# Moving an SBUF layout from multiples of 32 bytes to multiples of 64: four graph layers on one core

## The reference

```python
# layer 0, twice: relational convolution, 8 relations over 4 bases
m = sum(comp[etype, b] * norm * (h @ basis[b])[src] for b in bases)
out = segment_sum(m, dst) + bias + h @ loop_w
# layer 1: the same form, 32 relations over 8 bases
# layer 2: mean of the neighbours through W2, own row through W1
# layer 3, 4 blocks of:
y = (x - mu) * rsqrt(var + eps) * (1 + cond @ sw + sb) + cond @ bw + bb
q, k, v = y @ wq + bq, y @ wk + bk, y @ wv + bv     # 4 heads of 128
x = x + softmax_over_edges(q[src] . k[dst]) v[dst] @ wo + bo
y = norm(x) as above with its own weights
x = x + relu(y @ m_w1 + m_b1) @ m_w2 + m_b2
```

## Time and profile before

| | |
|---|---|
| median of three runs | 3153.47 us (3148.95, 3153.47, 3154.17) |
| profiled execution, first to last instruction (span) | 3143.3 us |
| PE busy | 94% of the span |
| VectorE, ScalarE, GpSimd busy | 66%, 41%, 38% |
| mean granted clock | 0.988 |

### The profile page before, as it was taken

The page is one execution under the profiler, slowest core; times in us unless marked ns, Lnnn a source line. Parts: engine busy times, 40 slices in busy tenths (PEclk is TensorE's granted clock), DMA queues, the critical chain, the costliest instruction groups (busy, mean ns, idle before and its releaser), DMA issues.

```text
span 3143.3 us, 42911 instructions
## 1 busy us (share of the span) xinstructions
PE 2966.4 (94%) x14658; PEld 2176.8 (69%) x14658; DVE 2076.1 (66%) x5081; ACT 1275.2 (41%) x2245; POOL 1178.9 (38%) x938
## 2 busy tenths in 40 slices
PE   5898998999979899999999999999999999999999
PEld 2333774445843357875458998889987999879987
DVE  7999224886358763444376677567766776767677
ACT  4666431002340033342254554355543555435554
POOL 4666336664456643432022123511135102431022
PEclk8999999999989999999999999999999999999999
DMA  2555524664246542333012001310113001130012
GB/s 80 166 168 161 166 96 136 171 173 143 81 131 179 169 124 89 95 99 121 12 45 88 15 31 50 101 43 8 37 57 118 14 8 65 44 104 15 8 64 80
DMA packets 129593, 279.31 MB, mean 89 GB/s; under 512 B 22742, under 2 KB 45590, under 8 KB 128354
## 3 DMA queue, kind: packets, MB, share of 16 engines
q0 software_dynamic: 40320, 132.15, 14.8%
q1 hardware_dynamic: 87618, 141.76, 14.2%
q10 hardware_dynamic: 1440, 2.62, 0.2%
HBM read 227.85 MB, written 27.48 MB: 81 GB/s over the span
## 4 chain that ended last, share of the span: by engine, by line
PE 74%; DVE 13%; another core or an unknown queue 6%; ACT 3%; issue 2%; DMA 2%; POOL 1%; DVEq 0%; SPq 0%; POOLq 0%; ACTq 0%
PE bank L155 16%; PE bank L157 16%; PE bank L156 16%; PE bank L889 9%; PE bank L2545 5%; PE bank L2209 3%; PE bank L1849 2%; PE bank L860 2%; DVE G L996 2%; DVE onehot_dst L963 1%; DVE y_tile L2161 1%; DVE y_tile L2163 1%; DVE x_stats L2144 1%; DMA yT_lo<-yT_new_lo 1%
## 5 line engine op out<-in xcount | busy, mean ns | idle before, releaser
L889 PE MATMUL bank<-gathered,selector 128*128 x1328 | 641.5, 606 | 57.7 <-SPq L848 30.9
L996 DVE TENSOR_TENSOR G<-G,bank 128x512 f32 x664 | 450.4, 678 | 23.5 <-PE bank L889 23.3
L889 PEld LDWEIGHTS bank<-gathered,selector 128*128 128x128 f32 x1328 | 231.8, 192 | 303.8 <-issue 167.2
L2633 ACT CAST probT<-bank 128x512 fp32r<-128x512 f32 (+2 forms) x480 | 212.2, 515 | 263.0 <-PE bank L2545 262.1
L1510 POOL TENSOR_TENSOR weight_parts<-weight_ring,weight_parts 128x512 fp32r<-128x512 f32 x130 | 188.0, 1446 | 296.7 <-ACT weight_parts L1443 296.6
L2715 DVE CUSTOM_DVE_ANT_0 prob<-bank,count_by_src 128x512 f32<-128x512 f32 (+1 forms) x480 | 258.4, 589 | 58.8 <-PE bank L157 58.8
L1469 DVE TENSOR_TENSOR lhs_parts<-G,lhs_parts 128x640 fp32r<-128x640 f32 x122 | 102.3, 840 | 288.4 <-ACT lhs_parts L1441 288.2
L2641 DVE TENSOR_TENSOR probT<-bank,probT 128x512 fp32r<-128x512 f32 (+2 forms) x480 | 254.0, 585 | 52.1 <-ACT probT L2633 51.3
L870 ACT COPY G<-bank 128x512 f32<-128x512 f32 x160 | 82.3, 654 | 492.2 <-remote 405.2
L155 PE MATMUL bank<-weight_parts,lhs_parts 128*128 128x512 f32 x680 | 268.7, 395 | 11.3 <-POOL weight_parts L1510 5.5
L157 PE MATMUL bank<-weight_parts,lhs_parts 128*128 128x512 f32 x680 | 266.5, 392 | 0.0
(11 more groups left out here) (295 smaller groups left out, 6807.5 us busy)
## 6 DMA issues: line engine op xcount, KB each, us to landing
weight_ring<-in_L_gnn_basis SPq DMA_DIRECT2D x64, 256.0 KB, 2.7
weight_ring<-in_L_gnn_bases SPq DMA_DIRECT2D x64, 256.0 KB, 2.7
x_L<-x_rows SPq DMA_DIRECT2D x50, 256.0 KB, 4.4
x_rows<-x_L SPq DMA_DIRECT2D x50, 256.0 KB, 5.8
yT_hi<-yT_new_hi SPq DMA_DIRECT2D x4, 2560.0 KB, 11.4
yT_lo<-yT_new_lo SPq DMA_DIRECT2D x4, 2560.0 KB
count_rows<-count SPq DMA_DIRECT2D x10, 642.0 KB, 5.7
count_by_dst<-count_rows SPq DMA_DIRECT2D x10, 642.0 KB, 4.6
```

The lines of the kernel that those rows point to most:

```text
L889: ins = pe.matmul(bank[s % banks][:], sel[:, s % SELECTORS, :], tile_rows_of[s % BATCH], start=True, stop=True)
L996: ins = dve.tensor_tensor(g, g, bank[s % banks][:], ALU.add)
L2633: ins = act.copy(hi, of)
```

## The change

The allocator rounds the start of every tensor of 256 bytes or more, and of every tensor made by `new_split`, up to a multiple of 64. `C.after_small` is rounded too. In layer 3 the ten tensors of small columns become slices of one tensor, `columns`, of 136 words per partition; `C.rows_place` becomes a multiple of 64, with probT first and prob behind it. `tile_of_step` and `steps_of_tile` (and the scratch `tile_int`) hold 2-byte instead of 4-byte entries; `window_of_step` stays at 4 bytes. No instruction is added, removed or reordered in the source.

```diff
 class Arena:
...
         self.n += 1
+        if size >= 256:
+            self.align()
         t = self.nc.alloc_sbuf_tensor_at(f"{name}_{self.n}", shape, dtype, offset=self.at)
...
+    def align(self):
+        self.at = -(-self.at // 64) * 64
+        return self.at
+
     def new_split(self, name, shape):
 
+        self.align()
         at = self.at
...
-    C.after_small = M.at
+    C.after_small = M.align()
...
-    C.tile_of_step = {PATH1: M.new("tile_of_step", [1, PATH1.steps // BATCH, 2, BATCH], I32)}
-    C.steps_of_tile = {PATH1: M.new("steps_of_tile", [1, T], I32)}
+    C.tile_of_step = {PATH1: M.new("tile_of_step", [1, PATH1.steps // BATCH, 2, BATCH], U16)}
+    C.steps_of_tile = {PATH1: M.new("steps_of_tile", [1, T], U16)}
...
-    C.tile_of_step[PATH0] = M.new("tile_of_step", [1, PATH0.steps // BATCH, 2, BATCH], I32)
-    C.steps_of_tile[PATH0] = M.new("steps_of_tile", [1, T], I32)
+    C.tile_of_step[PATH0] = M.new("tile_of_step", [1, PATH0.steps // BATCH, 2, BATCH], U16)
+    C.steps_of_tile[PATH0] = M.new("steps_of_tile", [1, T], U16)
...
-    tile_i = M.new("tile_int", [1, PATH1.steps], I32)
+    tile_i = M.new("tile_int", [1, PATH1.steps], U16)
...
-    C.rows_place = (M.end - 4 * (2 * N + 4 + 2 * NT * 4 * P)) // 32 * 32
+    C.rows_place = (M.end - 64 - 4 * (2 * N + 2 * NT * 4 * P)) // 64 * 64
...
-    stats = M.new("x_stats", [P, NT, 6])
-    means = M.new("x_mean_var", [P, NT, 2])
...
-    rsum = M.new("row_sum", [P, 2, NT])
+    columns = M.new("columns", [P, 10 * NT + 6 + KC + 6 + 2 * NT])
+    stats = columns[:, 0:6 * NT].rearrange("p (j a) -> p j a", a=6)
+    means = columns[:, 6 * NT:8 * NT].rearrange("p (j a) -> p j a", a=2)
...
+    hb, rmax, nmax = (columns[:, 10 * NT + 2 * a:10 * NT + 2 * a + 2] for a in range(3))
...
+    rsum = columns[:, 10 * NT + 12 + KC:].rearrange("p (h t) -> p h t", h=2)
...
-    prob = M.new("prob", [P, 2, N])
     PT = M.new("probT", [P, 2, 2, NT, QUERIES], F32R)
+    prob = M.new("prob", [P, 2, N])
```

More of the change, by code:

```diff
@@ L6 @@
 F32R = mybir.dt.float32r
-F32, I32, BF16, F16 = mybir.dt.float32, mybir.dt.int32, mybir.dt.bfloat16, mybir.dt.float16
+F32, I32, U16, BF16, F16 = mybir.dt.float32, mybir.dt.int32, mybir.dt.uint16, mybir.dt.bfloat16, mybir.dt.float16
 ALU = mybir.AluOpType
@@ L1966, in layer_3 @@
     modw = M.new("modulation_parts", [STACKED, 2, D], F32R)
-    stats = M.new("x_stats", [P, NT, 6])
-    means = M.new("x_mean_var", [P, NT, 2])
-    rstds = M.new("x_rstd", [P, NT, 1])
-    shifts = M.new("x_shift", [P, NT, 1])
-    hb = M.new("head_bias_cols", [P, 2])
-    mb = M.new("mlp_bias_cols", [P, KC])
-    rmax = M.new("row_max", [P, 2])
-    nmax = M.new("negated_max", [P, 2])
-    smax = M.new("span_max", [P, 2, 3])
-    rsum = M.new("row_sum", [P, 2, NT])
+    columns = M.new("columns", [P, 10 * NT + 6 + KC + 6 + 2 * NT])
+    stats = columns[:, 0:6 * NT].rearrange("p (j a) -> p j a", a=6)
+    means = columns[:, 6 * NT:8 * NT].rearrange("p (j a) -> p j a", a=2)
+    rstds = columns[:, 8 * NT:9 * NT].rearrange("p (j a) -> p j a", a=1)
+    shifts = columns[:, 9 * NT:10 * NT].rearrange("p (j a) -> p j a", a=1)
+    hb, rmax, nmax = (columns[:, 10 * NT + 2 * a:10 * NT + 2 * a + 2] for a in range(3))
+    mb = columns[:, 10 * NT + 6:10 * NT + 6 + KC]
+    smax = columns[:, 10 * NT + 6 + KC:10 * NT + 12 + KC].rearrange("p (s n) -> p s n", s=2)
+    rsum = columns[:, 10 * NT + 12 + KC:].rearrange("p (h t) -> p h t", h=2)
     V_hi = M.new("value_parts_hi", [P, 2, NP], F32R)
@@ L1987, in layer_3 @@
     M.at = heads_only = C.rows_place
+    PT = M.new("probT", [P, 2, 2, NT, QUERIES], F32R)
     prob = M.new("prob", [P, 2, N])
-    PT = M.new("probT", [P, 2, 2, NT, QUERIES], F32R)
     end_of_heads = M.at
```

## The result

The kernel after takes 3178.68 us (median of 6 runs, 3170.34 to 3185.15), the kernel before 3153.82 us beside it (6 runs, 3148.95 to 3161.01): ratio 1.0078, 95% interval 1.0063 to 1.0092. The forecast was 3145.5 us, faster than before, with a range of 3138.5 to 3154.5. The profiled execution of after took 3175.8 us and its span is 3174.4, 31.1 us more than before's. That is more than the 24.9 us between the medians. With the 1.4 us that lie around after's span, before's profiled execution took about 3144.7 us (an estimate), 9 us under the median of its kernel.

A forecast was written before the change was run, and what follows sets the result against it. PE was taken as the bound, busy 94% of the span, mostly split products in layer 3. PE's terms summed to -8.5 us; 90%, -8 us, from 3153.5 gave 3145.5 us, range 3138.5 to 3154.5.

The forecast's parts named there:

- Term 13: Two-byte tables, read as registers on PE and POOL in the gathers: same number of loads, taken at 0.
- register loads get dearer: Rival, PE's queue in the three gathers: dearer 2-byte loads make the kernel slower, 3170 us at 15% coming through; chance 0.06.
- Terms 1, 2 and 3: Layer 3's 512-wide projections from yT, value projections and hidden layer: aligning the one odd operand gains 3.5, 2.9 and 2.5 us.
- Terms 4 and 5: Layer 3's output products and 512-wide scores, both operands odd: alignment saves 3.1 ns per matmul, 3.0 us each.
- Term 6: Modulation by condT, 160 matmuls with both operands odd: gain between 0 and 1.1 us, taken as -0.5 us.
- Term 7: 256-wide matmuls: aligned pairs are slower, +5.6 us at the value products and +0.8 us at projections from yT.
- Term 8: The 226-wide matmuls, some 1300: between -3.5 and +3.8 us, taken as +0.5 us.
- Term 9: fp32 products (gathers, transposes, layer 2): G, gathered and selector stay at multiples of 64, bounds 0 either side.
- Term 10: ScalarE's 512-wide casts, 590 to 570 ns when aligned: beside PE, so taken as 0, with -1 us as other end.
- Terms 11 and 12: Copies (PE's 3.1 us wait for yT_lo) and the shared tensor of small columns: both taken at 0.
- the prediction's own signs of being wrong: Wrong if the gain lies outside layer 3, or layer 3 shortens by under 4 or over 12 us.
- address is not the cause: Rival: 227 against 233 ns hangs on relative place or SBUF row and survives the shift; 3153.5 us, no change; chance 0.18.

The follow-up runs named there:

- align_only: The kernel after with its tables put back to 4 bytes and one more register operation before PE's and POOL's waits against loaded values: ratio 1.0014 to before.
- held: The kernel before, 4-byte tables, with one more register operation in front of each PE and POOL wait against a loaded value: ratio 1.0019 to before.

## Why the prediction was wrong

- **Term 13, the tables, is the step that failed in size and sign of the whole.** It took 0, "since a load of four values stays one instruction". It does stay one, but lasts 985 ns instead of 329. The tables alone cost 1.4% on one chip, and PE's alone about 1% on another. The rival "register loads get dearer" had the place (PE's queue in the gathers), its sign came true (the gathers grow and PE's idle time is put down to issue), and at 15% coming through it had 3170 us. That this is only 9 us off is partly luck. It supposed loads twice as long, which would be 332 x 329 ns = 109 us more, and worked with 167 us, an idle time and not a load time; the loads became three times as long, 218 us more, and 14% of that came through. Its chance of 0.06 rested on the count of instructions and on VectorE's table staying at 4 bytes. The rows of 4-byte loads were in the trace and bound them at 329 ns; one load per value at the worst would have been 4 x 329 ns, 1.3 us, which is above what came.
- **Terms 1, 2 and 3** (8.9 us together for one odd operand) failed in cause. The distances went from 233.2 to 233.0, 233.3 to 232.4 and 233.2 to 232.6 ns, under 1 us in sum. The 6 ns were real, but belong to two operands whose rests by 256 differ; a shift that leaves them different keeps them. The rows at 227 ns had both tensors at the same rest by 256, not merely both at 64: 192 for yT_new and head_weights, and in the transforms weight_parts and lhs_parts both at 128 in layer 0 and both at 64 in layer 1.
- **Terms 4 and 5** (3.1 ns for both odd): 229.9 to 229.7 and 230.8 to 230.9. These pairs agree by 256 before and after and still are not at 227; in the trace most of their distances lie between 224 and 236. What lengthens them is open, and so is whether the rule is all that counts inside the kernel.
- **Term 6** (modulation, -0.5 us) is too small to be read. The 48 distances under 300 ns that the trace has before give 236.5 ns, the 44 after 233.2; but four over 260 ns make that difference, and without them it is 233.5 and 233.2.
- **Term 7** (+6.4 us) had the wrong sign: 117.4 to 116.6 ns at the value products, -1.6 us, and 117.3 to 115.3 at the projections. The shift of probT against V_hi and V_lo changed their rests (224 against 192 and 224, then 128 against 64 and 0); that this is the cause was not shown. **Term 8** (+0.5): 111.5 to 111.7 ns, right. Term 9: 429 ns as before, right.
- **Term 10**: the cast stays at 590 ns; the 20 ns against the cast into yT_new are not the address. It was taken at nothing for the end, so no harm was done. **Terms 11 and 12** at 0: PE's wait for yT_lo is 3.2 instead of 3.1 us, and align_only, which has the shared columns, is no slower than held.
- **The sum** of what layer 3 gained is 3.5 us, and was taken as 8; under 4 us was one of the prediction's own signs of being wrong. The rival "address is not the cause" named the tensors' place relative to each other, which is what was found at 512 columns; it was weighed at 0.18 against rows that could not tell the two apart, since every aligned pair in them was also an agreeing one. The Trainium skill's "Advanced Engine Details and Errata", section SBUF Cachelines, has lines of 16 bytes, from which the prediction worked out that 32 against 64 does nothing. The runs agree in that both operands 32 bytes on cost nothing, and that a moving operand 4 bytes on is the slowest (236.9 ns); the 6 ns between rests by 256 are not in that rule.

## What to carry to other kernels

Before an index table is narrowed, ask who reads it: as a register load, four 4-byte values cost PE 334 ns and four 2-byte values 984. Where an engine's queue is near full, a part of the time of its register loads comes through to the end (14% of 218 us here), and single register operations in front of its waits cost too (0.2% in held). In this kernel one load of eight 4-byte values with the operations packed behind it gave that back. For split products of 512 columns compare the rests by 256 of the two operands' addresses, not each address alone (4 to 5 us of 3092 and 3144 here). A correlation read from a trace should be checked on a pair that separates the candidates, and a few series on zeros do that in one run. And a stretch of one profiled execution should be compared with its busy time and clock before its length is explained: the third gather's 6.7 us were mostly neither of the change's two parts.

## What the runs showed that was not expected

- A register load costs by the value (some 235 ns each on PE), but four 4-byte values go as one: 334 ns, and eight 589 ns. The steps are the same on every engine (300 to 347 ns for four, 523 to 596 for eight).
- The stationary and the moving operand of an fp32r matmul interact by 256 bytes: 226.6 to 227.7 ns per 512 columns when their rests agree, 229 to 234 at other multiples of 32; at 256 columns it turns round, 120 ns when they agree and 113.3 to 118.8 at other multiples of 32; at 226 columns nothing (111.7).
- The chips differ by 2% on the same kernel (3091 and 3153 us), in the profiled executions 45 of 47 us of it in the second and third gather (held against before), and the cost of an edit in the gathers differs with it.
- The granted clock of a gather differs between executions of one kernel: the lower level held for 18.1 us in the third gather of one profiled execution of after and for 6.6 us in another, with 294.3 and 288.4 us.
